# A vision layer on one core: the key projection of each attention step directly behind the query projection

## The reference

```
h = layernorm_gamma(patches @ W)                      # embedding, 256 wide
x = layernorm(h)
q, k = silu(x @ Wq), silu(x @ Wk);  v = x @ Wv        # 16 heads of 64
cum = cumsum(-softplus(x @ Wa + ba))
attn[i, j] = (q_i . k_j) * exp(cum_i - cum_j), j <= i
o = groupnorm(attn @ v) * gn_w + gn_b                 # over a head's tokens and columns
h = h + (o * sigmoid(x @ Wg)) @ Wo
h = h + top-2 of 8 experts (256 -> 1024 -> 256, gelu) # per token, weighted
```

## Time and profile before

| | |
|---|---|
| median of three runs | 1324.96 us (1321.25 to 1325.42) |
| profiled execution | 1323.79 us, span 1321.9 us |
| PE busy | 1250.9 us, 95% of the span |
| ACT, DVE, POOL busy | 858.5, 825.2, 428.1 us |

### The profile page before, as it was taken

One profiled execution on the slowest core, in us unless ns is written; L12 is line 12 of the kernel. 1 busy time (PEld: TensorE's weight loads), 2 busy tenths in 40 slices (PEclk: granted clock), 3 DMA queues, 4 the chain that ended last, 5 costly groups with the idle time before them and its releaser, 6 DMA issues. The chain is left out here.

```text
span 1321.9 us, 27298 instructions
## 1 busy us (share of the span) xinstructions
PE 1250.9 (95%) x8534; PEld 1072.3 (81%) x8534; DVE 825.2 (62%) x2119; ACT 858.5 (65%) x2019; POOL 428.1 (32%) x524
## 2 busy tenths in 40 slices
PE   3899999999999999999999999999999999999996
PEld 2676777878778778778778778889999999989996
DVE  4455556665665665665665566657788888565552
ACT  2557577576576576576576565636788888666662
POOL 2021211241241241241141142164444544433434
PEclk7799999999999999999999999999999999999998
DMA  5321331341331331341332236458888787888873
GB/s 193 121 93 61 105 98 47 117 131 46 117 129 49 109 128 57 108 130 57 108 114 63 89 102 186 161 179 245 282 238 222 222 237 188 262 257 262 249 232 88
DMA packets 125607, 194.46 MB, mean 147 GB/s; under 512 B 16272, under 2 KB 91504, under 8 KB 125360
## 3 DMA queue, kind: packets, MB, share of 16 engines
q1 hardware_dynamic: 111920, 175.91, 41.5%
q0 software_dynamic: 13584, 17.26, 6.4%
HBM read 167.40 MB, written 29.05 MB: 149 GB/s over the span
## 5 line engine op out<-in xcount | busy, mean ns | idle before, releaser
L1161 PE MATMUL bank<-xn_sp,big_r 128*128 128x512 f32 x1152 | 312.1, 408 | 0.0
L1161 PEld LDWEIGHTS bank<-xn_sp,big_r 128*128 128x128 f32 x1152 | 204.6, 188 | 53.2 <-issue 1.4
L1674 DVE TENSOR_TENSOR att<-bank,dec_x 128x384 f32<-128x384 f32 x256 | 130.7, 552 | 110.1 <-PE bank L1198 108.9
L817 ACT ACTIVATE dec_x<-dec_x,ncum 128x256 f32<-128x256 f32 (+1 forms) x512 | 189.7, 444 | 5.7 <-POOL dec_x L654 5.7
L654 POOL TENSOR_SCALAR_AFFINE_SELECT dec_x<-dec_x 128x256 f32<-128x256 f32 x256 | 103.6, 434 | 215.8 <-DMA dec_x<-cum_scratch 215.7
L1494 PE MATMUL bank<-big_r 128*128 128x256 f32 x1296 | 168.0, 286 | 1.5 <-ACT mid_f L887 1.0
L1494 PEld LDWEIGHTS bank<-big_r 128*128 128x128 f32 x1296 | 160.5, 192 | 3.3 <-ACT mid_f L887 1.4
L705 POOL TENSOR_SCALAR mid_f<-mid_f,dec_x 128x256 f32<-128x256 f32 x71 | 76.9, 1087 | 187.0 <-DVE mid_f L1925 184.6
L711 POOL DMA_INDIRECT out<-mid_f,tok x71 | 118.6, 1671 | 53.0 <-POOL mid_f L705 22.0
L1941 DVE TENSOR_TENSOR big_r<-mid_f,big_r 128x256 fp32r<-128x256 f32 x216 | 91.4, 424 | 69.5 <-ACT big_r L907 69.3
L887 ACT ACTIVATE mid_f<-bank,h 128x256 f32<-128x256 f32 x216 | 101.2, 477 | 43.5 <-PE bank L1494 22.1
(11 more groups left out here) (217 smaller groups left out, 2231.4 us busy)
## 6 DMA issues: line engine op xcount, KB each, us to landing
big_f<-in_L_ffn_w SPq DMA_DIRECT2D x68, 1024.0 KB, 6.2
dec_x<-cum_scratch SPq DMA_DIRECT2D x128, 384.0 KB, 3.5
big_w<-in_L_ffn_w SPq DMA_DIRECT2D x12, 1024.0 KB, 6.7
mid_f<-expert_rows SPq DMA_DIRECT2D x27, 261.0 KB, 3.4
xt<-in_x SPq DMA_DIRECT2D x16, 256.0 KB, 3.7
h_scratch<-h SPq DMA_DIRECT2D x16, 256.0 KB, 2.3
h<-h_scratch SPq DMA_DIRECT2D x8, 512.0 KB, 4.3
out<-h SPq DMA_DIRECT2D x16, 256.0 KB, 4.0
```

Source lines behind the costliest of these rows:

```text
L817: act.activation(d, d, ACT.Exp, bias=ncum[p % 2][:, NS * u + s, 2 * c + hh:2 * c + hh + 1]).then_inc(M["exp_done"], 1)
L1161: mm = pe.matmul(bank[target][:, :], wp[:, k, c * P:(c + 1) * P], xp[:, k, :], start=(k == 0 and j == 0), stop=(k == EC - 1 and j == 2))
L1674: dve.tensor_tensor(att[hh][:, :], bank[4 + hh][:, 0:LW], dec[n % RING][:, hh, :], ALU.mult).then_inc(M["mult_done"], 1)
```

## The change

In each step of the pairs keys(c+1) stands directly behind queries(c+1) and the values of that step, ahead of weighted(c,0). On ACT tanh_k follows the first four exponentials. On DVE silu_k follows silu_q. In step 0 the two value tiles change their banks (2 and 1 become 1 and 2) with the waits that go with it. The last step of each pair (c = 7) is as it was.

```diff
--- before.py
+++ after.py
@@ -944,7 +944,10 @@
                 if main:
                     tanh_q(p, c + 1)
                     decay(p, c + 1, 0)
-                    for i, source in {0: ((2, 2), (3, 1)), 1: ((4, 2),), 3: ((7, 2),)}.get(c, ()):
+                    if c == 0:
+                        keep_v(p, 2, 1)
+                    tanh_k(p, c + 1)
+                    for i, source in {0: ((3, 2),), 1: ((4, 2),), 3: ((7, 2),)}.get(c, ()):
                         keep_v(p, i, source)
                 if c in (1, 2) and post:
                     affined(p - 1, 1, c - 1)
@@ -954,8 +957,6 @@
                     softplus(p + 1)
                 if c == 6 and main:
                     affined(p, 0, 0)
-                if main:
-                    tanh_k(p, c + 1)
                 if c == 6 and post:
                     keep_x2(2 * p - 1)
                 if main:
@@ -1174,14 +1175,14 @@
                 if p == 0 and c == 0:
                     pe.wait_ge(M["ws_lo"], 3)
                 have(pe, "sk_done", NP * p + c)
-                have(pe, "v_done", 2 * TP * p + {1: 4}.get(c, 0))
+                have(pe, "v_done", 2 * TP * p + {1: 3}.get(c, 0))
                 project(1, 1, c, "k_ps")
 
             def gates(p, c):
                 if p == 0 and c == 0:
                     pe.wait_ge(M["ws_lo"], 4)
                 have(pe, "tg_done", NP * p + c)
-                have(pe, "v_done", 2 * TP * p + {0: 1, 1: 3, 2: 5, 4: 8}.get(c, 0))
+                have(pe, "v_done", 2 * TP * p + {0: 1, 1: 4, 2: 5, 4: 8}.get(c, 0))
                 project(2, 3, c, "g_ps")
 
             def scores(p, c, u):
@@ -1363,12 +1364,13 @@
                     scores(p, c, 0)
                     queries(p, c + 1)
                     if c == 0:
-                        values(p, 2, 2, "tg_done", NP * p + 1)
-                        values(p, 3, 1, "sk_done", NP * p + 1)
+                        values(p, 2, 1, "sk_done", NP * p + 1)
+                        values(p, 3, 2, "tg_done", NP * p + 1)
                     if c == 1:
                         values(p, 4, 2, "tg_done", NP * p + 2)
                     if c == 3:
                         values(p, 7, 2, "tg_done", NP * p + 4)
+                    keys(p, c + 1)
                 if c == 0 and post:
                     gn_mean(p - 1, 1, "h2a_done", 2 * p - 1)
                 if c == 1 and routed:
@@ -1386,7 +1388,6 @@
                 if main:
                     weighted(p, c, 0)
                     scores(p, c, 1)
-                    keys(p, c + 1)
                 if c == 0 and post:
                     gn_var(p - 1, 1)
                 if c == 1 and nxt:
@@ -1985,6 +1986,7 @@
                     if c > 0:
                         head_stats(p, c - 1)
                     silu_q(p, c + 1)
+                    silu_k(p, c + 1)
                 if c == 0:
                     if post:
                         spread(p - 1, 1)
@@ -2011,8 +2013,6 @@
                     decayed(p, c, 1)
                 if c == 4 and post:
                     residual(2 * p - 2)
-                if main:
-                    silu_k(p, c + 1)
                 if c == 0:
                     if post:
                         affine(2 * p - 1)
```

## The result

| | before | after |
|---|---|---|
| median | 1325.19 us (1321.25 to 1327.13, 4 runs) | 1345.77 us (1345.27 to 1346.34, 4 runs) |
| ratio | | 1.0159 (95%: 1.0135 to 1.0183) |
| profiled execution | 1323.79 us, span 1321.9 | 1345.27 us, span 1343.3 |

The change makes the kernel slower by 1.6%, 20.6 us; 1342 was predicted, in a range of 1332 to 1353.

The account below looks back on a forecast made before the run. PE's instruction stream was taken to bound the attention stage. The terms 8.3 + 1.3 + 2.7 + 0.5 + (5.1 + 1.45 - 0.3) - 1.2 gave 17.9 us slower, taken as 1342, range 1332 to 1353.

Parts of the forecast that it names:

- Step 5: Pairs 1 to 6: new PE wait of 1.45 at gn_var, +0.85 each; pair 7 +1.45, pair 0 -0.3.
- Step 0: Spread and choose behind silu_k delay decayed(0,1): +1.34 each in pairs 2 to 6; sum 8.3, including pair 7's step 1.
- Step 1: Pairs 0 and 1, without rank matmuls between keys and turn: norm late by 0.65 each, +1.3.
- Step 3: Norm and turn late behind decayed(3,1): +0.43 each in pairs 1 to 6, pair 0 -0.3, pair 7 +0.45; sum 2.7.
- Step 6: Waits for products behind the late step 5 go: -0.8 in pair 0, under 0.1 in each other, -1.2 in all.
- Steps 2 and 4: Step 2 has room for the placing; in pair 7's step 4 the second output projection waits 0.5 for the residual.
- the expert stage: The part from 831 us on, claimed to be the same before and after.
- PE's busy time: Sign in the profile after: it stays near 1251 us, with the clock in the pairs at 1.00.
- The clock rival: The granted clock also falls around seven new step 5 waits of 1.45: 12 us more, 1354; chance 0.09.
- step 7: Last step of each pair: not touched, and the 8.0 us of waits for keep_o stay.
- The faster rival: DVE work behind silu_k still ends inside the gate projection; waits for issue and turn go: -9.6, 1315; chance 0.05.
- No change: Rival: PE's work is the same and the small gains and losses meet; 1324; chance 0.07.

Follow-up runs that it names:

- fourth experiment: The changed kernel with the expert choice (choose) of step 0 moved behind decayed(0,1) on DVE, the kernel with the late choice; 1341.85 us.
- first experiment: The changed kernel with silu_k on DVE moved back behind decayed(c,1), PE and ACT as changed; 1319.61 us.
- second experiment: The kernel before, PE's order kept, with silu_k directly behind silu_q on DVE and tanh_k behind the first exponentials and all value copies on ACT; 1460.03 us.

## Why the prediction was right, and where it was off

- **The mechanism is shown.** DVE takes its instructions in order, and silu_k waits there for PE and ACT with other work behind it. With the same instructions on all three engines, taking that one operation back removes the loss (1345.77 to 1319.61). That the sum came so near is partly luck: several terms below are off by a microsecond or more, and their errors partly cancel.
- **Step 5** was sized well: a wait of 1.45 predicted and 1.45 measured, +0.85 each and 0.89 measured, +1.45 in pair 7. The miss is pair 7, +3.05. The wait there is 1.45 too; the other 1.6 are slower matmuls (below).
- **Step 0** was sized well in pairs 2 to 6, 1.34 predicted and 1.38 to 1.48 measured (pair 1: 0.45 and 0.54); gn_var's wait of 0.4 is 0.32. In pair 7 steps 0 and 1 together are +2.02 and not +1.1: the keys ahead of the wait for the routing tables did not give back what was counted. The fourth experiment takes 1.1 us off the wait in that step 1, so choose had a hand in it; the chain wasn't followed further.
- **Step 1** of pairs 0 and 1 was placed too high, 0.65 each predicted, 0.40 and 0.54 measured, and pairs 2 to 6 gave 0.1 each that was not counted.
- **Step 3** is the term of the sum that was too large, 2.7 for 1.55. These are DVE and PE there, answering to the earlier trace rows:

```profile
291.93 0.69 DVE L1666 SCALAR_TENSOR_TENSOR k_s<-tq,bank 128x512 f32<-128x512 f32 x1 [2.06 <-ACT tq L794]
292.53 1.22 DVE L1723 TENSOR_TENSOR y_sp<-big_f,y_sp 128x1024 fp32r<-128x1024 f32 x1
...
294.60 0.72 DVE L1618 TENSOR_SCALAR turned<-h,st1u,rs 128x256 f32<-128x256 f32 x2
```

```profile
295.47 0.63 PE L1123 MATMUL bank<-ident,turned 128*128 128x128 f32 x4 [0.95 <-DVE turned L1618]
```

  From silu_k to the norm there are 2.67, which is what the prediction had (287.52 to 290.19). But silu_k itself came 0.24 earlier in its step than placed, so turn is 0.17 late and not 0.43. In pair 7 it is 0.98 and not 0.45. There PE waits 0.21 for the products and 0.36 for keep_v; the rest no row shows as idle. The wait for keep_v came by a path that the prediction had set aside with "SP and POOL keep their order": ACT's exponentials wait for POOL's masks (line 654). On POOL these stand behind the gathers of routed rows (line 676), which wait for DVE and start 1.5 us later against the step than before. In the first experiment, with ACT's order the same, that wait is absent.

```profile
801.77 1.03 POOL L676 DMA_INDIRECT expert_rows<-xn,slot  x1 [7.30 <-DVE slot L1810]
...
807.41 1.49 ACT L817 ACTIVATE dec_x<-dec_x,ncum 128x256 f32<-128x256 f32 x4 [1.51 <-POOL dec_x L654]
```

- **Step 6** gave 1.8 and not 1.2. Pair 0 gave the 0.85 that it was counted for. The others are 0.2 shorter each instead of under 0.1, in pieces that no row shows as idle. They are as short in the first experiment, so this comes with PE's order and not with silu_k.
- **Steps 2 and 4** came near what was placed (0.15 for 0, and 0.49 for 0.5 in pair 7), and **the expert stage** is the same within 0.7 us: the loss lies ahead of 852 us.
- **PE's busy time** was to stay near 1251 us and is 1260.6. Some 3 us of that are the two low clocks below; the rest is spread, and the prediction had no term for it.
- **The clock rival** (1354) had its mechanism half right. It happened in one of seven step 5's with a wait of 1.45, and cost 1.6 us there, close to the 1.7 taken from the earlier trace rows. A step 7 that the prediction left out lost 1.35 in pair 6 to a low clock as well. Without these two the sum by steps would be 16.9, so the waits by themselves were predicted 1 us too high, and a clock that the sum did not have made up for it.
- **The faster rival** (1315) is refuted for the order as changed. Part of its gain is there to be had when silu_k's place is left alone: 1319.61, with the wait for "issue" gone but turn's grown.
- **No change** is refuted by the ratio's interval.

## What to carry to other kernels

When a producer is moved earlier, its consumer on an in-order engine shouldn't move along by habit: put it behind all that doesn't need it and that somebody waits for, and just ahead of its deadline. Here one operation placed too early on an engine that is only 61% busy cost 26 us, and left where it was it lets the rest of the change gain 4 (over 1 of that by the clock in one step). Look for the mirror case as well: an operation that waits for nothing new, as the norm in step 3, belongs in front of the operation that waits; that was worth 8 us with no other change.

## What was not expected of the hardware

The granted clock did not answer to the length of a wait alone. In the changed kernel, pair 2 and pair 7 have the same wait of 1.45 us ahead of gn_var. The first two rows are pair 7 on PE, then come a stretch of pair 2 and one of pair 7, columns as in the earlier trace rows:

```profile
834.19 0.39 PE L1227 MATMUL bank<-gt,half 128*128 128x8 f32 x2 [1.45 <-DVE gt L1694]
834.44 2.02 PE L1162 MATMUL bank<-xn_sp,big_r 128*128 128x512 f32 x5
```

```profile
318.00:323.00 5.00, 3.71 (x28) 2.89 (x28) 3.15 (x13) 4.96 (x10) 2.38 (x3) 1.00 0.26 82
...
835.00:837.00 2.00, 2.00 (x7) 1.50 (x6) 0.25 (x3) 0.08 (x1) 1.75 (x2) 0.50 0.48 135
```

Pair 2 kept 1.00, that is 2.4 GHz, and its six matmuls took 1.63. In pair 7 the clock was 0.50, the level of 1.2 GHz, and five took 2.02. In the kernel with the late choice the same wait did it in pair 2 as well:

```profile
318.61 0.39 PE L1227 MATMUL bank<-gt,half 128*128 128x8 f32 x2 [1.45 <-DVE gt L1694]
318.85 2.48 PE L1162 MATMUL bank<-xn_sp,big_r 128*128 128x512 f32 x6
```

```profile
318.00:323.00 5.00, 4.39 (x18) 3.19 (x20) 2.50 (x10) 3.88 (x8) 2.38 (x3) 0.66 0.28 80
```

Its DMA share is 0.28 against 0.26, and PE has the same matmuls, so these rows show nothing that would tell the two apart. Pair 7 lost it in both profiles of the changed kernel, and in the one with the late choice. The Trainium skill, "TensorE: Matmul & The Clock Gate", section "A second HAM failure mode: psum-queue depth-cycling", says that short idle times between groups of matmuls can make the clock swing between its two rates; these rows agree that a wait of 1.45 can be enough, and show that mostly it is not. What decides stays open. In the second experiment, with waits of up to 3.0 us, the mean clock from the first scores to the last was 0.95, where it was 1.00 in the kernel before. An estimate from that: 5% of those 916 us are 46 us, most of the 59 by which PE's busy time rose.

The step 7 of pair 6 holds an old wait of 3.21 us for keep_o. The clock in the 8 us from its end on, in the changed kernel:

```profile
746.80:754.80 8.00, 8.00 (x34) 5.59 (x36) 4.39 (x7) 1.90 (x3) 2.30 (x6) 0.61 0.89 290
```

and in the kernel before:

```profile
732.80:740.80 8.00, 7.97 (x40) 5.71 (x41) 4.90 (x7) 3.24 (x7) 3.10 (x6) 0.79 0.88 293
```

The mean clock is lower in the changed kernel, and the step is 1.35 us longer with its order untouched. In the three other profiles with the keys moved on PE and silu_k ahead of the products on DVE it is 1.0 to 1.2 us longer than before; in the four with silu_k in its old place it is within 0.15 of before. Such a long wait is thus a place where a change elsewhere can move a microsecond.

Finally, a wait that goes gives back some more than the profile shows as idle: 0.95 for 0.76 at turn, and 0.63 for 0.53 at the scores. The ends of matmuls are modelled, so that idle time is counted from a modelled end, which may be why; no run tested it.
